# A routed-expert decoder layer: sentinel rows in place of a table fill, tile assignment ahead of the last shared pieces, and a routing probability by tanh

## What is computed

```
x = x + attn(layernorm(x))             # gated linear recurrence over each sequence, two small projections
x = x + xattn(ctx, layernorm(x))       # per sequence: dynamic time warping, ctx rows added along the path
x = x + ffn(layernorm(x))

ffn: shared = swiglu(x, sw1, sw2, sw3)                    # hidden size 352
     probs  = sigmoid(clip(x @ router_w.T + bias, -50, 50))   # 7 experts
     p, sel = top_k(probs, 1)                             # one expert per token, the first of equals
     y      = swiglu(x, ew1[sel], ew2[sel], ew3[sel])
     out    = 0.5 / (0.5 + p) * shared + p * y / (0.5 + p)
```

## Time and profile before

| | us |
|---|---|
| median of 3 runs | 341.24 (341.22 to 341.62) |
| the profiled execution | 340.31 |
| its span from first to last instruction | 338.6 |
| PE busy | 234.7 (69%) |
| DVE busy | 201.6 (60%) |
| POOL busy | 154.2 (46%) |
| ACT busy | 146.1 (43%) |

### The profile page before, as it was taken

How to read it: one execution, slowest core, us unless ns; L and a number is a source line. 1 busy time by engine, 2 the same in 40 slices (tenths; PEclk the granted TensorE clock), 3 DMA queues, 4 the chain that set the end, 5 groups by cost and what they waited for, 6 DMA issues and landing times.

```text
span 338.6 us, 5303 instructions
## 1 busy us (share of the span) xinstructions
PE 234.7 (69%) x1301; PEld 171.6 (51%) x1301; DVE 201.6 (60%) x809; ACT 146.1 (43%) x382; POOL 154.2 (46%) x227
## 2 busy tenths in 40 slices
PE   1186688963000002698989999995399999999993
PEld 1034366863000002664647665663277877868772
DVE  0579999760699985435769657535244444535441
ACT  2475676652710204629393663220044344343441
POOL 7366777465000000311117677640026766757666
PEclk9999999998555555569999999999699999999999
DMA  8999101222599999999981122221214444434531
GB/s 213 314 350 388 48 17 32 63 63 56 134 205 147 144 172 254 195 140 139 158 167 38 59 86 78 80 70 32 61 39 53 60 56 52 63 42 62 62 36 8
DMA packets 63324, 37.56 MB, mean 111 GB/s; under 512 B 8272, under 2 KB 60624, under 8 KB 63184
## 3 DMA queue, kind: packets, MB, share of 16 engines
q10 hardware_dynamic: 30872, 15.71, 31.5%
q1 hardware_dynamic: 25928, 17.29, 18.0%
q0 software_dynamic: 6496, 4.24, 9.2%
HBM read 14.53 MB, written 22.94 MB: 111 GB/s over the span
## 4 chain that ended last, share of the span: by engine, by line
PE 23%; POOL 15%; issue 9%; DVE 6%; ACT 5%; DMA 3%; SPq 0%; POOLq 0%; ACTq 0%; DVEq 0%
POOL out L982 15%; PE bank L746 6%; PE bank L757 5%; PE bank L759 4%; PE bank L653 3%; ACT pay L667 2%; DMA xs<-routed 2%; DVE mk L650 2%; DVE bn L158 1%; DMA out<-loan,xs 1%; PE bank L908 1%; DVE xr L657 1%; ACT mk L645 1%; PE bank L909 1%; ACT xT L675 1%
## 5 line engine op out<-in xcount | busy, mean ns | idle before, releaser
L982 POOL DMA_INDIRECT out<-loan,xs x38 | 58.8, 1547 | 53.2 <-issue 29.0
L167 POOL TENSOR_TENSOR rstds<-ve,half 128x4 f32<-128x4 f32 x24 | 27.7, 1154 | 55.7 <-DVE ve L165 52.9
L966 DVE TENSOR_TENSOR loan<-bank,loan 128x352 f32<-128x352 f32 x38 | 19.9, 525 | 38.1 <-PE bank L909 38.1
L737 POOL DMA_INDIRECT routed<-pay,pos_i x32 | 31.5, 986 | 15.2 <-issue 6.4
L950 ACT COPY h_ffn<-bank 128x256 f32<-128x256 f32 x38 | 14.2, 373 | 47.2 <-PE bank L934 47.2
L924 PE MATMUL bank<-w_sb,h_ffn 128*128 (+1 forms) x228 | 31.9, 276 | 1.4 <-ACT h_ffn L951 1.4
L924 PEld LDWEIGHTS bank<-w_sb,h_ffn 128*128 128x128 f32 (+1 forms) x228 | 28.6, 191 | 7.5 <-issue 7.0
L761 ACT ACTIVATE loan<-bank 128x512 f32<-128x512 f32 (+1 forms) x24 | 14.2, 595 | 41.1 <-PE bank L757 32.2
L908 PE MATMUL bank<-w_sb,xsT 128*128 x76 | 29.7, 473 | 0.0
L909 PE MATMUL bank<-w_sb,xsT 128*128 x76 | 29.3, 468 | 0.0
L769 DVE TENSOR_TENSOR h_ffn<-bank,loan 128x512 f32<-128x512 f32 (+1 forms) x24 | 16.4, 689 | 20.3 <-PE bank L759 10.7
(11 more groups left out here) (203 smaller groups left out, 554.6 us busy)
## 6 DMA issues: line engine op xcount, KB each, us to landing
routed<-fill ACTq DMA_DIRECT2D x1, 14950.0 KB, 88.5
w_sb<-in_w SPq DMA_DIRECT2D x8, 352.0 KB, 8.0
xs<-routed SPq DMA_DIRECT2D x38, 65.0 KB, 2.1
xr<-in_x SPq DMA_DIRECT2D x8, 256.0 KB, 5.8
cn<-in_ctx SPq DMA_DIRECT2D x8, 256.0 KB, 6.2
cT<-in_ctxT SPq DMA_DIRECT2D x8, 256.0 KB, 6.1
out<-xr SPq DMA_DIRECT2D x8, 256.0 KB, 2.4
w_sb<-in_w SPq DMA_DIRECT2D x8, 192.0 KB, 10.0
```

Of the source, the lines that this page charges most:

```text
L167: return pool_done(pool.tensor_tensor(rstds[:, k, s], ve[:, k, s], half[:, s], ALU.pow))
L737: pool.indirect_dma_start(routed, bass.IndirectOffsetOnAxis(ap=pos_i[:, n:n + 1], axis=0), pay[:, n, :], None, bounds_check=TABLE - 1).the ...
L966: dve.tensor_tensor(g[:, i, 0:HID], U[i][:, 0:HID], g[:, i, 0:HID], ALU.mult).then_inc(s_h, 1)
L982: pool.indirect_dma_start(out_rows, bass.IndirectOffsetOnAxis(ap=xs[:, s % XB, ROW - 1:ROW].bitcast(U32), axis=0), y[:, s % 4, :], None, b ...
```

## The change

1. The table fill goes. An expert's range becomes 4096 + 128 rows (`CAP`). Six spare tiles behind the ranges are filled by one small DMA from SP (393 KB), and behind each expert's last row a DMA from SP writes 128 sentinel rows (7 DMAs of 65 KB), at a row number that SP reads from `fill_at`. The tile loads wait for those eight DMAs. Tiles past the last expert now lie in the spare tiles.
2. The tile assignment becomes a generator of three parts, advanced between the last pieces of the shared expert, as soon as the last round has its row numbers.
3. The loop advances the chunks in two half turns and puts a piece of the shared expert between them; the round's parts stand at other places between the pieces.
4. The probability is 0.5 * tanh(0.5 * logit) + 0.5 instead of a sigmoid; the expert is chosen by min(logit, 0) + probability, so that DVE has three more small operations per round.

```diff
-TABLE = NE * TOK + (NS - NT) * P
+CAP = TOK + P
+TABLE = NE * CAP + (NS - NT) * P
...
-            after(act, m_tri)
-            m_fill = load(act, routed.rearrange("(k p) r -> p k r", p=P), fill[:, None, :].to_broadcast([P, TABLE // P, ROW]), "fill_out")
+            after(sp, m_tri)
+            spare = routed[NE * CAP:, :].rearrange("(k p) r -> p k r", p=P)
+            m_spare = load(sp, spare, fill[:, None, :].to_broadcast([P, NS - NT, ROW]), "spare_out")
...
-            m_pr = mark("prob", r, act_done(act.activation(pr[:, :, :], lg[:, :, :], ACT.Sigmoid)))
+            m_pr = mark("prob", r, act_done(act.activation(pr[:, :, :], lg[:, :, :], ACT.Tanh, scale=0.5)))
             yield
             after(dve, m_pr, old("rank", r - 1))
+            chain(dve.tensor_scalar(pr[:, :, :], pr[:, :, :], 0.5, 0.5, ALU.mult, ALU.add))
+            chain(dve.scalar_tensor_tensor(t1[:, :, :], lg[:, :, :], 0.0, pr[:, :, :], ALU.min, ALU.add))
+            chain(dve.tensor_reduce(km[:, :], t1[:, :, :], AX_X, ALU.max))
+            chain(dve.tensor_tensor(oh[:, :, :], t1[:, :, :], over_e(km), ALU.is_equal))
             chain(dve.tensor_reduce(pm[:, :], pr[:, :, :], AX_X, ALU.max))
-            chain(dve.tensor_tensor(oh[:, :, :], pr[:, :, :], over_e(pm), ALU.is_equal))
...
-                after(pool, old("pos", n // GT), old("norm", n // CT), m_fill if n == 0 else None, m_id if n == 0 else None)
+                after(pool, old("pos", n // GT), old("norm", n // CT), m_id if n == 0 else None)
...
+        def assign_tiles():
+            after(pe, old("pos", NG - 1))
+            m = pe_done(pe.matmul(TOTAL, ones[:, :], before_t[:, :, GT], start=True, stop=True))
+            yield
...
+            m_end = chain(dve.tensor_copy(fill_at[:, 0:NE], TOTAL[0:1, :]))
...
-            under_way = [gen for gen in under_way if next(gen, "end") != "end"]
-            if turn >= 6 and turn % 2 == 0:
-                router = route((turn - 6) // 2)
-            if router:
+            under_way = advance(under_way)
+            if turn >= 7 and turn % 2:
                 next(router)
             put_rows(3 if turn <= NC + 2 else NT)
-            if turn >= 5:
+            if turn >= 6:
                 next(expert)
-            if router and turn % 2:
+            under_way = advance(under_way)
+            if turn >= 7 and turn % 2:
                 next(router)
             if turn >= 5:
                 next(expert)
-            if router and turn % 2:
+            if turn >= 7 and turn % 2:
                 next(router, None)
+            if turn >= 6 and turn % 2 == 0 and turn < 2 * NG + 5:
+                router = route((turn - 6) // 2)
+                next(router)
         put_rows(NT)
+        assign = assign_tiles()
         while next(expert, "end") != "end":
-            pass
+            next(assign, None)
...
             row_reg = [sp.alloc_register(f"tile_row{k}") for k in range(4)]
-            for c in range(NC - 1):
+            fill_reg = [sp.alloc_register(f"fill_row{k}") for k in range(NE)]
+            for c in range(4):
+                store_x3(c)
+            after(sp, m_end)
+            sp.load(fill_reg, fill_at[0:1, 0:NE])
+            for e in range(NE):
+                base = sp.snap(fill_reg[e], min_val=e * CAP, max_val=e * CAP + TOK)
+                sp.dma_start(routed[bass.ds(base, P), :], fill[:, :]).then_inc(s_end[e], 16)
+            for c in range(4, NC - 1):
                 store_x3(c)
             sp.wait_ge(s_put, NT * 16)
-            after(sp, m_rows)
+            after(sp, m_rows, m_spare, *((s_end[e], 16) for e in range(NE)))
```

More of the change, by code:

```diff
@@ L610, in program @@
         lt = room.take(NE, NT)
-        ekc, skc = (room.take(NS, NE - 1, parts=1) for _ in range(2))
-        ekf, started_at = (room.take(NS, parts=1) for _ in range(2))
+        ekc, skc = (room.take(NS, NE, parts=1) for _ in range(2))
+        ekf, ekr, started_at = (room.take(NS, parts=1) for _ in range(3))
         mk = sb("mk", [P, 2, CT, P])
@@ L644, in aligned @@
             for t in range(CT):
-                m = act_done(act.activation(mk[:, b, t, :], iota_f[:, :], ACT.Abs, bias=middle[:, c * CT + t:c * CT + t + 1]))
+                m_abs = act_done(act.activation(mk[:, b, t, :], iota_f[:, :], ACT.Abs, bias=middle[:, c * CT + t:c * CT + t + 1]))
             yield
-            after(dve, m, m_reach)
+            yield
+            after(dve, m_abs, m_reach)
             for t in range(CT):
@@ L650, in aligned @@
                 m_mk = dve_done(dve.tensor_scalar(mk[:, b, t, :], mk[:, b, t, :], reach[:, n:n + 1], None, ALU.is_le))
+            yield
             after(pe, m_mk, old("x2", c - 2))
             for t in range(CT):
[L653 to L654 removed]
+                m_al = pe_done(pe.matmul(ALIGN[b][:, t * D:(t + 1) * D], mk[:, b, t, :], cn[:, c * CT + t, :], start=True, stop=True))
+            mark("al", c, m_al)
             yield
[L656 removed]
+            after(dve, m_al)
             m_x2 = mark("x2", c, dve_done(dve.tensor_tensor(xr[:, s, :], ALIGN[b][:, :].rearrange("p (t d) -> p t d", d=D), xr[:, s, :], ALU.add)))
@@ L668, in aligned @@
             mark("norm", c, m_n)
+            yield
             after(pe, m_n, old("xT", c - 1))
             for t in range(CT):
-                m = pe_done(pe.transpose(X_T[:, t * P:(t + 1) * P], pay[:, c * CT + t, 0:D], ident[:, :]))
+                m_t = pe_done(pe.transpose(X_T[:, t * P:(t + 1) * P], pay[:, c * CT + t, 0:D], ident[:, :]))
             yield
             a = slice(c * CW, (c + 1) * CW)
-            after(act, m)
+            after(act, m_t)
             m_xT = mark("xT", c, act_done(act.copy(xT[:, a], X_T[:, :])))
+            yield
             after(pe, m_xT, m_rt, old("pos", c // 2 - 1))
@@ L866, in program @@
         s_o = [sem(f"tile_put{k}") for k in range(4)]
+        s_end = [sem(f"end_fill{e}") for e in range(NE)]
         out_rows = out.rearrange("b t d -> (b t) d")
```

47 lines of the change are left out of this document (26 added, 21 removed).

## The result

The changed kernel took **329.68 us** (median of 4 runs, 329.09 to 330.58) beside 341.43 us for the kernel before in the same comparison: a ratio of 0.9657, 95% interval 0.9629 to 0.9684. In a later comparison it was 0.9695 [0.9655, 0.9736]. The prediction was 331.7 us with a range of 327.8 to 335.0. The profiled execution took 330.12 us for a span of 328.9.

The account below looks back on a forecast made before the run. PE was taken to bound the last two stages, idle only from 234.3 to 242.0 us. From 340.3 us, 7.7 (joint) and 1.8 (stage 3) came off and 0.9 (median) went on: 331.7 us, range 327.8 to 335.0.

Parts of the forecast that it names:

- joint: Between the last `down_all` and stage 4's first tiles: hiding the tile assignment and load saves 7.7 us, bounds 5.5 to 8.9.
- stage 3: Router rounds and shared expert: the new order of pieces saves 1.8 us, bounds -1.5 to 4.5.
- the stall in stage 4: One late tile load in stage 4 costing 0.9 us, which may or may not recur; left in the forecast.
- the median: Whole kernel: the median of the runs was 0.93 us above the profiled execution; 0.9 us added at the end.
- The fill and its DMAs: Table fill and its small replacements on SP: no gain taken (bound 1 us), the new DMAs costed at nothing.
- The walk: Queues walked from 148.2 us at earliest starts: PE waits 1.8 us in round 0; chunk 3's `down_all` ends at 198.8.
- The tanh: Router rounds: no table loads in stage 3, ACT does 10.3 us less; DVE's three more operations cost 0.75 us a round.
- Round 3: PE stands 2.8 us for a multiply behind the chain; `down_all` of chunk 3 to the next 11.7 us, giving back 2.6.
- the clock falls in round 3: Rival: PE's 2.8 us wait in round 3 lowers its clock, adding 1.8 to 2 us: 333.6 us; chance 0.06.
- The signs: Right: last `down_all` ending near 232, among others; wrong: chunk 3's after 201 or granted clock under 1 between 160 and 240.
- the forecast's own case: Whole kernel: time as worked out, 329.5 to 333.3 us; chance 0.54.
- the joint alone: Rival: DVE is in the way in every round, stage 3 gives 0 to -1.5 us: 333.3 to 335; chance 0.20.

Follow-up runs that it names:

- joint_only: Kernel before with only the tile assignment moved, in three parts between the last pieces of the shared expert: 332.18 us, ratio 0.9757.
- joint_undone: Changed kernel with the tile assignment (all but `fill_at`) held back until the shared expert's last piece is through: 339.18 us, ratio 0.996.
- tanh_undone_again: Changed kernel with the sigmoid and the former choice of expert back, run again on another chip: 330.68 us.
- tanh_only: Kernel before with the tanh's lines and nothing else changed: 338.63 us, ratio 0.9954.
- fill_back: Changed kernel with one fill of the whole table from ACT's queue instead of the eight small ones: 341.15 us, ratio 0.9852.
- after_again: Changed kernel as it is, run again in a later comparison: 330.66 us.
- spare_late: Changed kernel with SP's fill of the spare tiles held until ACT's last square root in stage 2: 328.25 us, ratio 0.9647.
- mult_first_r3: Changed kernel with the shared expert's piece ahead of the router's step in the loop's last round alone: 326.79 us, ratio 0.9602.
- warm_r3: Changed kernel with 16 products of unused result on PE behind round 3's rank products: 341.51 us, ratio 0.9858.
- tanh_undone: Changed kernel with the sigmoid and the former choice of expert back: 340.62 us, ratio 0.9832.
- both: Changed kernel with the spare tiles' fill late and the shared expert's piece ahead of the router's step in every round: 336.38 us, ratio 0.9727.

## Why the prediction was right in size, and where it was wrong

The forecast of 331.7 us missed by 2.0, and its two main terms were both off. From the prediction's 331.7: joint 1.2 us more, stage 3 1.8 less, the stall in stage 4 0.8 to 0.9 more, 0.5 more from what lies around the span (1.7 us before, 1.2 after), and 1.4 from the median. That is 2.1, so 329.6. Five terms of 0.5 to 1.8 us that partly cancel make a miss of 2.0, and so close a hit is in part luck.

- **The joint.** The gap behind the last `down_all` was put at 1.6 us and measured 1.5; loads ahead of the end of `down_all`, clock at 1.00, two transposes waiting for nothing but their bank. Right, and shown by `joint_only` and `joint_undone`. Mis-sized was the fill of the pipeline behind it: one tile of 1.8 us plus one of 2.29. The first tiles have neither a down product nor a transpose back among their products yet, so the steps were 1.39 and 1.62 us (235.75, 237.14, 238.76). The joint gave 8.9 us for 7.7.
- **The fill and its DMAs, "at nothing".** For the large fill and the seven sentinel DMAs this held. For the spare fill it failed: "on SP, where no one is waiting" looked at SP's queue and not at the loads that ACT's queue had in flight. All of stages 2 and 3 began 0.9 us later.
- **The order, rounds 0 to 2.** The walk said 198.8 for chunk 3 and it was 199.2 from a start 0.9 us later; its wait in round 0 was put at 1.8 us and measured 1.82. The numbers were right. The reason given ("since ACT has no loads") was wrong: with the loads back, chunk 3 ends even earlier (198.2, `tanh_undone_again`), and without them in the old order it ends as late as before (204.3, `tanh_only`).
- **The tanh.** ACT's 10.3 us were taken as the cover for item 3's gain, and are worth 0.0 us in the runs of the changed order. The three added DVE operations, put at 0.75 us a round, cost 0.70 (the chain of round 0 takes 3.71 us for 3.01), and lie on the path in round 0, since a multiply is queued behind them.
- **Round 3.** The wait was put at 2.8 us and measured 0.81 + 2.06. The step c3 to c4 was put at 11.7 us and measured 13.7. That took the whole 1.8 us that the forecast gave to stage 3. The rival "the clock falls in round 3", with a price of 1.8 to 2 us and a chance of 0.06, came true: 0.50 from 208 to 210. The forecast had leaned on waits of up to 2.8 us in stage 1 that had left the clock at 1.00. A wait of that length did not prove harmless elsewhere. What decides is not shown: in round 0 a wait of 1.85 us behind one of 0.34 brought the fall (`fill_back`), and one of 1.82 alone did not. The Trainium skill (TensorE: Matmul & The Clock Gate, Part 1) says that an array that idles falls back to half rate. The trace agrees here, and not in round 0 of the changed kernel, where PE waited 1.82 us and the clock stayed at 1.00.
- **The median.** The profiled run of before was the fast end of its runs, 0.93 under the median; that of after lay 0.44 above its own. Carrying the offset over cost 1.4 us, as much as a mechanism.
- **The signs.** Those of the joint came as named. The last `down_all` was to end near 232 and ended at 234.2, and a granted clock under 1 from 160 to 240, named as a sign of being wrong, did show.

So the time fell where the forecast's own case had it, but by two cases at once (the joint alone, and the fallen clock) and a larger joint.

## What to carry to other kernels

When a serial chain must share an in-order engine with a producer that PE waits for, put the producer ahead of the chain: here one exchange in one round gave back part of the wait and, with it, the clock, 3.5 us by the traces and 2.9 by the medians. Taking work off an engine pays where others wait for it while it has work in hand; with 10 us of loads gone, `tanh_only` shows PE's waits for ACT unmoved. And a DMA put on an idle queue can still delay the small transfers of another queue that someone awaits, so look at what is in flight at that moment.

## What the runs showed that I had not expected

- **The clock in round 3.** Idle stretch (below) apart, it fell in every trace in which PE's two waits (0.8 to 1.5 and 2.1 to 2.2 us) stood there (after, `after_again`, `spare_late`, `joint_undone`, `tanh_undone_again`), and in neither of those with one wait of 1.5 us. A wait like it isn't a sure cause: in round 0 such a wait brought the fall in `fill_back` and not in after, and in `joint_only` the clock fell at about 164 where the kernel before, with the same instructions there, kept it. It also rises at a different moment after stage 2: it reached 1.00 between 149 and 153 us, 1.2 to 4.1 us behind the first product of the shared expert. In six traces of one and the same order (after, `after_again`, `mult_first_r3`, `spare_late`, `joint_undone`, `warm_r3`) c0 ends 19.3 to 19.9 us behind that product, the later the later the rise: 0.6 us.
- **Late tile loads in stage 4.** Single steps of 2.4 to 3.7 us instead of 2.29 turn up at another tile in twelve of the fourteen traces (from 254 to 314 us), from none to two of them a run. A term taken from one of them is noise.
- **An idle stretch that stays open.** In four kernels that ran beside each other (`fill_back`, `warm_r3`, `tanh_undone`, `both`), on a chip where the kernel before took 347.23 us instead of 341, DVE and ACT both stood idle at the same place, where DVE takes up round 2's rank products, with no releaser that the trace names. In `warm_r3`:

```profile
201.41 0.25 DVE L739 TENSOR_TENSOR loan<-bank,picked 128x56 f32<-128x56 f32 x1 [4.94 <-remote]
201.45 0.60 ACT L777 ACTIVATE loan<-bank 128x512 f32<-128x512 f32 x1 [6.57 <-remote]
```

5 to 9.5 us each, and 10 to 12 us on the total. PE waited 4.4 to 5.9 us for ACT behind it and then ran at 0.50. `tanh_undone` and `both` run again on another chip did not have it, so the code isn't its cause alone. What held the two engines I don't know. The times of these four are therefore compared with each other only.
